# Causal attention in a fused transformer layer: one exp over a pair of key blocks

## The chip, the cores and the metric

The kernel runs on eight NeuronCores of one Trainium2 chip, each with one sequence of the batch. A core has a matmul engine (TensorE, PE in the profile, PEld for its weight loads), a vector engine (DVE), a scalar engine for activations (ACT), GpSimd (POOL), SyncE (SP), which issues DMAs, SBUF as working memory and PSUM with eight banks of 512 float32 columns per partition. Engines run their own queues in order and meet at semaphores. The metric is the device time in microseconds of the slowest core.

## What is computed

```python
def attn(x, W_query, W_key, W_value):          # x is layer-normed, 8 x 2048 x 1024, H = 16 heads, DH = 64
    q, k, v = ...                              # projections, split into heads
    scores = jnp.einsum('bhqd,bhkd->bhqk', q, k)
    scores = jnp.where(causal, scores, -jnp.inf)
    weights = jax.nn.softmax(scores / jnp.sqrt(jnp.float32(DH)), axis=-1)
    ctx = jnp.einsum('bhqk,bhkd->bhqd', weights, v)
    return ctx.transpose(0, 2, 1, 3).reshape(b, n, H * DH)

x = x + attn(layernorm(x), W_query, W_key, W_value)
x = x + ffn(layernorm(x), w1, conv_w, conv_b, w2)   # quantized linear, depthwise conv, silu, quantized linear
```

Each core works on one sequence of 2048 tokens.

## The kernel before

A first stage normalizes x and makes `qT`, `kT` and `vaug` (the values with a column of ones, which yields the row sums of softmax). The attention stage follows, from about 390 to 1010 us. The last stage is the feed-forward part.

In attention the loop over t (lines from 770) takes four query tiles of 512 rows; for tile t there are KC = 4t + 4 key blocks of 128. Within t, `hp` takes eight pairs of heads. For each key block `kc`, TensorE makes the scores of both heads with two matmuls (64 rows each, in the two halves of the array) into one half of the PSUM tensor `psS4`: `psS[kc % 2]`, two banks of four. ACT applies exp to this half (1024 columns, fewer on the four diagonal blocks, where columns above the diagonal are left out) and writes to `PT` in SBUF. The scores of kc wait for the exp of kc - 2, which read the same half. The first scores of a head pair also wait for the last matmuls of the previous pair's product with the values, and stand behind them on TensorE's queue.

After the exps of a head pair, DVE multiplies the diagonal blocks by a mask (eight instructions), TensorE multiplies `PT` by `vaug` into `psPV` (called PV here; 52, 84 and 116 matmuls for t = 1, 2, 3), and DVE divides by the row sums and adds to `x1st`, the residual rows of tile t. `x1st` is loaded by GpSimd's queue at the start of t and stored at its end; one buffer serves all tiles, so the load waits for the store.

Between head pairs `emit_wsteps(2)` adds two steps of the work on the feed-forward weights, in a fixed order: 16 steps of abs with a sum on ACT for w1, a finalize step (DVE and TensorE), 16 steps of abs for w2, another finalize step, then 16 + 16 steps of quantization on DVE (three instructions each). Each step has its own load into `wbuf` on SyncE's queue. A quantization step also stores its result on this queue, behind its own arithmetic and ahead of the load of the next step. Two steps a head pair put w1's abs into t = 0, w2's into t = 1, and quantization from head pair 1 of t = 2 on; two last steps come after the loop.

Every instruction goes through `Eng.emit` (line 75 in the profile). ACT and DVE have `chain=True`: each of their instructions waits for the end of the one before on its engine.

Of the kernel before, what the change touches and what calls it, by code (L numbers as in the profile page):

```python
# [10 lines left out]
AF = mybir.ActivationFunctionType  # L11
# [10 lines left out]
QTW = 512  # L22
# [109 lines left out]
def build_program(debug=False):  # L132
# [39 lines left out]
    with es:  # L172
# [14 lines left out]
        smalls = es.enter_context(nc.sbuf_tensor("smalls", [128, 64], F32))  # L187
# [7 lines left out]
        SE = Eng(nc.scalar, s_a, chain=True)  # L195
# [3 lines left out]
        toks = {}  # L199
# [12 lines left out]
        sec_s = sec("scalar")  # L212
# [237 lines left out]
        with esA2:  # L450
            PT = esA2.enter_context(nc.sbuf_tensor("PT", [128, 4 * 16 * 512], BF16))
            PTW = 16 * 512
# [5 lines left out]
            psS4 = esA2.enter_context(nc.psum_tensor("psS4", [128, 2048], F32))  # L458
# [313 lines left out]
            for t in range(NQT):  # L772
# [15 lines left out]
                for hp in range(8):  # L788
                    hA, hB = 2 * hp, 2 * hp + 1

                    for kc in range(KC):
                        hpar = kc % 2

                        @sec_t
                        def _(te, t=t, hp=hp, kc=kc, hpar=hpar, KC=KC,
                              q0=q0):
                            if kc >= 2:
                                TE.wait(toks[("exp", t, hp, kc - 2)])
                            elif hp >= 1:
                                TE.wait(toks[("exp", t, hp - 1, KC - 2 + kc)])  # L800
                            elif t >= 1:
                                TE.wait(toks[("exp", t - 1, 7, 4 * t - 2 + kc)])
                            if kc == 0:
                                if hp >= 1:
                                    TE.wait(toks[("pv", t, hp - 1, 1)])
                                elif t >= 1:
                                    TE.wait(toks[("pv", t - 1, 7, 1)])
                            TE.wait(toks["qkv_done_v"])
                            bP = psS[hpar]
                            TE.emit("matmul", bP[:, 0:QTW],  # L810
                                    kT[0:64, hp * S + 128 * kc:hp * S + 128 * (kc + 1)],
                                    qT[0:64, hp * S + q0:hp * S + q0 + QTW],
                                    start=True, stop=True,
                                    tile_position=(0, 0),
                                    skip_group_check=True)
                            TE.emit("matmul", bP[:, QTW:2 * QTW],
                                    kT[64:128, hp * S + 128 * kc:hp * S + 128 * (kc + 1)],
                                    qT[64:128, hp * S + q0:hp * S + q0 + QTW],
                                    start=True, stop=True,
                                    tile_position=(64, 0),  # L820
                                    skip_group_check=True)
                            toks[("sc", t, hp, kc)] = TE.tok()

                        @sec_s
                        def _(se, t=t, hp=hp, kc=kc, hpar=hpar, q0=q0):
                            SE.wait(toks[("sc", t, hp, kc)])
                            SE.wait(toks["expbias"])
                            if kc == 0:
                                if hp >= 2:
                                    SE.wait(toks[("pv", t, hp - 2, 0)])  # L830
                                    SE.wait(toks[("pv", t, hp - 2, 1)])
                                elif t >= 1:
                                    SE.wait(toks[("pv", t - 1, 6 + hp, 0)])
                                    SE.wait(toks[("pv", t - 1, 6 + hp, 1)])
                            c0 = max(0, (kc - 4 * t) * 128)
                            bP = psS[hpar]
                            src_ap = bP[:].rearrange(
                                "p (h w) -> p h w", w=QTW)[:, :, c0:QTW]
                            PTp = PT[:, (hp % 2) * 2 * PTW:
                                      (hp % 2 + 1) * 2 * PTW]  # L840
                            dst_ap = PTp.rearrange(
                                "p (h w) -> p h w", w=16 * 512)[
                                :, :, 512 * kc + c0:512 * (kc + 1)]
                            toks[("exp", t, hp, kc)] = SE.emit(
                                "activation", out=dst_ap, in_=src_ap,
                                func=AF.Exp, scale=0.125,
                                bias=smalls[:, 6:7])

                    PTp_A = PT[:, (hp % 2) * 2 * PTW:
                               (hp % 2) * 2 * PTW + PTW]  # L850
                    PTp_B = PT[:, (hp % 2) * 2 * PTW + PTW:
                               (hp % 2 + 1) * 2 * PTW]

                    @sec_v
                    def _(ve, t=t, hp=hp, PTp_A=PTp_A, PTp_B=PTp_B):
                        for j in range(4):
                            kc = 4 * t + j
                            VE.wait(toks[("exp", t, hp, kc)])
                            for P in (PTp_A, PTp_B):
                                sl = P[:, 512 * kc + 128 * j:512 * kc + 128 * (j + 1)]  # L860
                                VE.emit("tensor_tensor", sl, sl, maskt[:],
                                        ALU.mult)
                        toks[("mask", t, hp)] = VE.tok()

                    for hi, (head, P) in enumerate(((hA, PTp_A),
                                                    (hB, PTp_B))):
                        pv = psPV[hi]

                        @sec_t
                        def _(te, t=t, hp=hp, hi=hi, head=head, P=P, pv=pv):  # L870
                            if hp >= 1:
                                TE.wait(toks[("epi", t, hp - 1, hi)])
                            elif t >= 1:
                                TE.wait(toks[("epi", t - 1, 7, hi)])
                            TE.wait(toks[("exp", t, hp, 4 * t + 3)])
                            TE.wait(toks[("mask", t, hp)])
                            first = True
                            for m in range(4):
                                for kc in range(4 * t + m + 1):
                                    last = (m == 3) and (kc == 4 * t + 3)  # L880
                                    TE.emit(
                                        "matmul", pv[:, VW * m:VW * m + VW],
                                        P[:, 512 * kc + 128 * m:512 * kc + 128 * (m + 1)],
                                        vaug[:, kc * H * VW + head * VW:
                                             kc * H * VW + (head + 1) * VW],
                                        start=first, stop=last,
                                        skip_group_check=True)
                                    first = False
                            toks[("pv", t, hp, hi)] = TE.tok()

                        @sec_v
                        def _(ve, t=t, hp=hp, hi=hi, head=head, pv=pv,
                              xpar=xpar):
                            VE.wait(toks[("pv", t, hp, hi)])
                            VE.wait(toks[("x1_load", t)])
                            rs = pv[:, 0:4 * VW].rearrange(
                                "p (m w) -> p m w", w=VW)[:, :, DH:DH + 1]
                            VE.emit("reciprocal", recb[:, 0:4], rs)
                            for m in range(4):
                                xsl = x1st[:, m * D + head * DH:  # L900
                                           m * D + (head + 1) * DH]
                                VE.emit("scalar_tensor_tensor", xsl,
                                        pv[:, VW * m:VW * m + DH],
                                        recb[:, m:m + 1], xsl,
                                        ALU.mult, ALU.add)
                            toks[("epi", t, hp, hi)] = VE.tok()

                    emit_wsteps(2)
# [633 lines left out]
```

How the kernel before makes its waits and increments, by code:

```python
    def wait(self, tok):  # L52
        if tok is None:
            return
        if isinstance(tok, list):
            for t in tok:
                self.wait(t)
            return
        sem, val = tok
        if val <= 0:
            return
        key = id(sem)
        if self._waited.get(key, -1) >= val:
            return
        if not DRY[0]:
            self.raw.wait_ge(sem, val)
        self._waited[key] = val
# [1 line left out]
    def emit(self, name, *a, waits=(), **kw):  # L69
        if self.chain and self.n > 0:
            self.wait((self.sem, self.n))
        for t in waits:
            self.wait(t)
        if not DRY[0]:
            inst = getattr(self.raw, name)(*a, **kw)
            inst.then_inc(self.sem, 1)
        self.n += 1
        return (self.sem, self.n)
# [20 lines left out]
    def wait(self, tok):  # L99
        if tok is None:
            return
        if isinstance(tok, list):
            for t in tok:
                self.wait(t)
            return
        sem, val = tok
        if val <= 0:
            return
        key = id(sem)
        if self._waited.get(key, -1) >= val:
            return
        if not DRY[0]:
            self.raw.wait_ge(sem, val)
        self._waited[key] = val
# [1 line left out]
    def emit(self, name, *a, waits=(), **kw):  # L116
# [5 lines left out]
        if not DRY[0]:  # L122
            inst = getattr(self.raw, name)(*a, **kw)
            inst.then_inc(self.sems[j], 16)
        self.counts[j] += 16
```

## Time and profile before

| | us |
|---|---|
| median of the runs | 2216.52 (2216.39 to 2216.64) |
| profiled execution | 2218.43 |
| its span, slowest core (core 1) | 2216.9 |
| spans of the eight cores | 2198.3 to 2216.9 |
| mean granted TensorE clock | 0.703 to 0.711 of full speed |

Busy shares of the span on core 1 are 50% for matmuls, 48% for DVE, 37% for ACT and 13% for GpSimd. A timeline row reads: start, duration, engine, instruction with what it writes and reads, its count, and in brackets how long the engine sat idle before it and what ended this. A row with a count merges instructions that follow each other, with the gaps between them in its duration.

### The profile page before, as it was taken

Reading aid. Unit: us, or ns where it says so; the run is one execution under the profiler, and the core shown is the slowest. Engines: PE = TensorE matmul, PEld = TensorE weight load, DVE = VectorE, ACT = ScalarE, POOL = GpSimd, SP = SyncE. Lnnn points to the kernel's source line nnn. Section 1 sums busy time; section 2 is a strip of 40 time slices with the busy share of each in tenths; the row PEclk is TensorE's granted clock in tenths of the full one; section 3 lists DMA queues with packets and bytes.
Section 4 is the critical chain, followed back from the end, with each engine's and each line's share of the span. In section 5 each row is a group of like instructions: output and inputs, shape, how many; then the busy total and the mean of one; then the engine's idle time right before and its main releaser. Section 6 shows DMA issues by size and latency. Waiting matters only on the chain.

```text
span 2216.9 us, 23771 instructions; the slowest of 8 cores (2198.3 to 2216.9 us)
## 1 busy us (share of the span) xinstructions
PE 1100.4 (50%) x7038; PEld 600.2 (27%) x7038; DVE 1058.7 (48%) x2042; ACT 829.2 (37%) x904; POOL 281.7 (13%) x255
## 2 busy tenths in 40 slices
PE   0666784435444345551032346447364373757655
PEld 0322330113222222221021223324233242344422
DVE  1344444423245555554454645636456465566660
ACT  3100000858654445661133253261532524352522
POOL 0000000000000000000011321313213122142420
PEclk9977895555655556665566668668787687878787
DMA  7211001564523353334722131321313213141400
GB/s 215 73 38 39 19 18 59 200 199 152 190 69 123 123 167 113 117 118 168 239 95 86 49 112 48 123 67 59 120 51 124 67 58 105 57 152 58 133 19 19
DMA packets 108273, 224.03 MB, mean 101 GB/s; under 512 B 4593, under 2 KB 70258, under 8 KB 104050
## 3 DMA queue, kind: packets, MB, share of 16 engines
q1 hardware_dynamic: 94962, 172.18, 24.1%
q0 software_dynamic: 13184, 50.34, 6.4%
q8 instruction: 58, 0.95, 0.2%
q14 instruction: 69, 0.57, 0.1%
HBM read 188.94 MB, written 33.55 MB: 100 GB/s over the span
## 4 chain that ended last, share of the span: by engine, by line
DVE 34%; PE 24%; DMA 15%; ACT 15%; issue 9%; DVEq 1%; SPq 0%; ACTq 0%; POOL 0%; POOLq 0%
PE psQK L75 8%; PE psO L75 6%; DVE amx L75 5%; DVE t1s L75 5%; PE psPV L75 4%; DVE hsil L75 4%; DVE smalls L75 4%; DMA wbuf<-w1t 4%; ACT PT L75 4%; PE psM L75 3%; ACT hf L75 3%; DMA x1t<-x1scr 3%; DVE tmpc L75 3%; DVE cbuf L75 3%; DMA wbuf<-w2t 2%
## 5 line engine op out<-in xcount | busy, mean ns | idle before, releaser
L75 PE MATMUL psM<-xqT,t1b 128*128 128x258 bf16 x2048 | 334.4, 334 | 363.8 <-DVE cbuf L75 355.7
L75 ACT ACTIVATE PT<-psS,smalls 128x1024 bf16<-128x1024 f32 (+1 forms) x320 | 315.5, 986 | 227.8 <-PE psS L75 198.3
L75 PEld LDWEIGHTS psM<-xqT,t1b 128*128 128x128 bf16 x2048 | 235.8, 119 | 461.5 <-issue 394.2
L75 ACT ACTIVATE tmpc<-psM,convb_s,convw_s 128x256 f32<-128x256 f32 x256 | 144.5, 565 | 385.9 <-PE psM L75 254.6
L75 PE MATMUL psS<-qT,kT 64*128 64x512 bf16 x640 | 174.2, 548 | 192.4 <-ACT PT L75 186.7
L75 PE MATMUL psO<-t2T,hq 128*128 128x512 bf16 x1024 | 225.0, 382 | 35.1 <-ACT hq L75 35.1
L75 DVE SCALAR_TENSOR_TENSOR tmpc<-psM,convw_s,tmpc 128x256 f32<-128x256 f32 x256 | 123.7, 483 | 233.2 <-ACT tmpc L75 211.6
L75 POOL TENSOR_TENSOR hsil<-cbuf,hsil 128x1024 f32<-128x1024 f32 x64 | 150.7, 2354 | 541.8 <-ACT hsil L75 541.8
L75 PE MATMUL psPV<-vaug,PT 128*128 128x65 bf16 x2176 | 113.6, 234 | 117.5 <-DVE PT L75 117.5
L75 ACT ACT_TABLE_LOAD x26 | 33.4, 1283 | 302.4 <-DVE smalls L75 174.7
L75 PEld LDWEIGHTS psPV<-vaug,PT 128*128 128x128 bf16 x2176 | 110.0, 126 | 132.7 <-issue 132.7
L75 PEld LDWEIGHTS psO<-t2T,hq 128*128 128x128 bf16 x1024 | 100.2, 98 | 158.6 <-issue 41.2
L75 DVE SCALAR_TENSOR_TENSOR cbuf<-psM,convw_s,tmpc 128x256 f32<-128x256 f32 x256 | 123.7, 483 | 27.1 <-DVE tmpc L75 0.5
L75 PEld LDWEIGHTS psS<-qT,kT 64*128 64x128 bf16 x640 | 38.5, 100 | 316.1 <-issue 316.1
L75 DVE TENSOR_REDUCE amx<-hsil 128x256 f32<-128x8192 f32 x8 | 112.7, 14088 | 4.7 <-POOL hsil L75 3.9
L75 DVE TENSOR_TENSOR PT<-PT,mask_s 128x128 bf16<-128x128 bf16 x256 | 57.6, 225 | 102.8 <-ACT PT L75 80.2
L75 DVE TENSOR_SCALAR t1s<-wbuf,smalls 128x2048 bf16<-128x2048 f32 x32 | 41.1, 1286 | 125.4 <-DMA wbuf<-w2t 62.1
L75 DVE TENSOR_TENSOR hsil<-hsil,s2row 128x256 f32<-128x256 f32 x128 | 92.5, 723 | 14.1 <-DVE hsil L75 0.9
L75 POOL TENSOR_TENSOR hsil<-hsil,s2row 128x256 f32<-128x256 f32 x128 | 93.9, 734 | 40.6 <-DVE s2row L75 22.4
L75 ACT ACTIVATE smalls<-smalls 128x1 f32<-128x1 f32 x64 | 13.0, 203 | 229.4 <-DVE smalls L75 225.9
L75 ACT ACTIVATE hsil<-cbuf 128x1024 f32<-128x1024 f32 x64 | 67.6, 1056 | 54.3 <-DVE cbuf L75 52.1
L123 POOL DMA_DIRECT2D x1scr<-x1st x4 | 3.8, 945 | 652.4 <-DVE x1st L75 652.4
(80 smaller groups left out, 1173.1 us busy)
## 6 DMA issues: line engine op xcount, KB each, us to landing
t1b<-t1scr SPq DMA_DIRECT2D x64, 1024.0 KB, 5.4
wbuf<-w1t SPq DMA_DIRECT2D x32, 1024.0 KB, 6.3
wbuf<-w2t SPq DMA_DIRECT2D x32, 1024.0 KB, 6.0
xstage<-x POOLq DMA_DIRECT2D x16, 512.0 KB, 3.6
x1st<-x POOLq DMA_DIRECT2D x4, 2048.0 KB, 10.3
x1scr<-x1st POOLq DMA_DIRECT2D x4, 2048.0 KB, 10.1
t1scr<-t1s SPq DMA_DIRECT2D x16, 512.0 KB, 3.4
t2scr<-t1s SPq DMA_DIRECT2D x16, 512.0 KB, 3.2
```

Of the source, the lines that this page charges most:

```text
L75: inst = getattr(self.raw, name)(*a, **kw)
L123: inst = getattr(self.raw, name)(*a, **kw)
```

## The change

For key blocks off the diagonal (kc + 1 < 4t), two neighbours are taken together. The scores of kc and kc + 1 are emitted one behind the other, in the same halves as before, and one exp over both halves (2048 columns, all four banks of `psS4`) waits for both and writes both blocks of `PT`. Both exp tokens are set to this one instruction. Diagonal blocks keep one exp each. There are 2, 4 and 6 such pairs in a pair of heads for t = 1, 2, 3, and none for t = 0.

```diff
-                    for kc in range(KC):
+                    def emit_sc(t, hp, kc, KC, q0):
                         hpar = kc % 2
...
+                    def emit_exp2(t, hp, kc):
+                        @sec_s
+                        def _(se, t=t, hp=hp, kc=kc):
+                            SE.wait(toks[("sc", t, hp, kc)])
+                            SE.wait(toks[("sc", t, hp, kc + 1)])
+                            exp_pvwaits(t, hp, kc)
+                            src_ap = psS4[:].rearrange(
+                                "p (x h w) -> p h x w", x=2, h=2, w=QTW)
+                            PTp = PT[:, (hp % 2) * 2 * PTW:
+                                      (hp % 2 + 1) * 2 * PTW]
+                            dst_ap = PTp.rearrange(
+                                "p (h w) -> p h w", w=16 * 512)[
+                                :, :, 512 * kc:512 * (kc + 2)]
+                            dst_ap = dst_ap.rearrange(
+                                "p h (x w) -> p h x w", w=QTW)
+                            tok = SE.emit(
+                                "activation", out=dst_ap, in_=src_ap,
+                                func=AF.Exp, scale=0.125,
+                                bias=smalls[:, 6:7])
+                            toks[("exp", t, hp, kc)] = tok
+                            toks[("exp", t, hp, kc + 1)] = tok
+
+                    kc = 0
+                    while kc < KC:
+                        if kc + 1 < 4 * t:
+                            emit_sc(t, hp, kc, KC, q0)
+                            emit_sc(t, hp, kc + 1, KC, q0)
+                            emit_exp2(t, hp, kc)
+                            kc += 2
+                        else:
+                            emit_sc(t, hp, kc, KC, q0)
+                            emit_exp1(t, hp, kc)
+                            kc += 1
```

`emit_sc` and `emit_exp1` hold the former body of the loop, with its waits; `exp_pvwaits` holds the waits of the exp for the bias and, at kc = 0, for the PV of two head pairs before.

## Rows read from the trace of the kernel before

**Rows 1.** The page, chain that ended last, shares by line.
```profile
PE psQK L75 8%; PE psO L75 6%; DVE amx L75 5%; DVE t1s L75 5%; PE psPV L75 4%; DVE hsil L75 4%; DVE smalls L75 4%; DMA wbuf<-w1t 4%; ACT PT L75 4%; PE psM L75 3%; ACT hf L75 3%; DMA x1t<-x1scr 3%; DVE tmpc L75 3%; DVE cbuf L75 3%; DMA wbuf<-w2t 2%
```

**Rows 2.** Windows: stretch, length, busy us of PE, PEld, DVE, ACT, POOL, clock, DMA.
```profile
484.00:583.00 99.00, 54.24 (x486) 28.04 (x486) 33.65 (x139) 81.87 (x85) 0.00 (x0) 0.55 0.38 134
824.00:1017.00 193.00, 97.43 (x1032) 51.20 (x1032) 99.32 (x170) 115.11 (x112) 0.00 (x0) 0.62 0.34 115
```

**Rows 3.** Waits of the attention stage, 392 to 1063 us: total, times, longest.
```profile
ACT PT L75 <- PE psS L75: 198.3, 24, 19.6
PE psS L75 <- ACT PT L75: 186.7, 256, 3.5
```

**Rows 4.** Timeline of head pair 3 in t = 1, all engines.
```profile
516.21 1.03 PE L75 MATMUL psS<-qT,kT 64*128 64x512 bf16 x4
516.97 8.32 ACT L75 ACTIVATE PT<-psS,smalls 128x1024 bf16<-128x1024 f32 x8 [0.67 <-PE psS L75]
518.23 0.61 PE L75 MATMUL psS<-qT,kT 64*128 64x512 bf16 x2 [0.99 <-ACT PT L75]
524.86 1.21 DVE L75 TENSOR_TENSOR PT<-PT,mask_s 128x128 bf16<-128x128 bf16 x4 [0.23 <-ACT PT L75]
526.22 3.02 PE L75 MATMUL psPV<-vaug,PT 128*128 128x65 bf16 x52 [1.56 <-DVE PT L75]
```

**Rows 5.** Groups of instructions by form, ACT, attention stage: count, busy us, mean ns.
```profile
L75 ACT ACTIVATE PT<-psS,smalls 128x1024 bf16<-128x1024 f32 x224 | 249.6, 1114 | 216.8 <-PE psS L75 198.3
L75 ACT ACTIVATE wbuf<-wbuf 128x2048 f32<-128x2048 f32 x32 | 61.1, 1910 | 9.3 <-DMA wbuf<-w1t 7.1
L75 ACT ACTIVATE PT<-psS,smalls 128x512 bf16<-128x512 f32 x32 | 22.0, 687 | 3.0
L75 ACT ACTIVATE PT<-psS,smalls 128x256 bf16<-128x256 f32 x32 | 15.2, 474 | 4.2
```

**Rows 6.** Timeline of PE in t = 2 and t = 3.
```profile
624.87 3.90 PE L75 MATMUL psPV<-vaug,PT 128*128 128x65 bf16 x84 [1.56 <-DVE PT L75]
...
650.73 4.55 PE L75 MATMUL psPV<-vaug,PT 128*128 128x65 bf16 x84 [8.60 <-DVE PT L75]
...
822.74 0.61 PE L75 MATMUL psS<-qT,kT 64*128 64x512 bf16 x4 [0.19 <-PE psPV L75]
824.56 0.39 PE L75 MATMUL psS<-qT,kT 64*128 64x512 bf16 x2 [1.21 <-ACT PT L75]
...
844.99 5.65 PE L75 MATMUL psPV<-vaug,PT 128*128 128x65 bf16 x116 [4.35 <-DVE PT L75]
```

**Rows 7.** Timeline of DVE and ACT in t = 1 and t = 2.
```profile
484.01 0.18 DVE L75 RECIPROCAL recb<-psPV 128x4 f32<-128x4 f32 x1 [14.35 <-DMA x1st<-x]
...
490.61 8.32 ACT L75 ACTIVATE PT<-psS,smalls 128x1024 bf16<-128x1024 f32 x8 [19.63 <-PE psS L75]
...
621.73 0.56 DVE L75 TENSOR_TENSOR PT<-PT,mask_s 128x128 bf16<-128x128 bf16 x2 [11.07 <-ACT PT L75]
...
629.61 13.15 ACT L75 ACTIVATE PT<-psS,smalls 128x1024 bf16<-128x1024 f32 x12 [5.67 <-PE psS L75]
...
648.05 2.53 DVE L75 TENSOR_TENSOR PT<-PT,mask_s 128x128 bf16<-128x128 bf16 x8
```

**Rows 8.** Timeline of DVE and ACT in t = 3.
```profile
808.40 1.29 DVE L75 TENSOR_SCALAR t1s<-wbuf,smalls 128x2048 bf16<-128x2048 f32 x1 [12.86 <-DMA wbuf<-w1t]
...
823.30 17.98 ACT L75 ACTIVATE PT<-psS,smalls 128x1024 bf16<-128x1024 f32 x16 [16.16 <-PE psS L75]
...
842.31 2.53 DVE L75 TENSOR_TENSOR PT<-PT,mask_s 128x128 bf16<-128x128 bf16 x8
...
848.51 0.18 DVE L75 RECIPROCAL recb<-psPV 128x4 f32<-128x4 f32 x1 [3.67 <-PE psPV L75]
...
1004.42 2.29 ACT L75 ACTIVATE PT<-psS,smalls 128x768 bf16<-128x768 f32 x3 [0.37 <-ACT PT L75]
...
1006.66 2.53 DVE L75 TENSOR_TENSOR PT<-PT,mask_s 128x128 bf16<-128x128 bf16 x8
```

More of the change, by code:

```diff
@@ L822, in _, with exp_pvwaits, emit_exp1 @@
                             toks[("sc", t, hp, kc)] = TE.tok()
+                    def exp_pvwaits(t, hp, kc):
+                        SE.wait(toks["expbias"])
+                        if kc == 0:
+                            if hp >= 2:
+                                SE.wait(toks[("pv", t, hp - 2, 0)])
+                                SE.wait(toks[("pv", t, hp - 2, 1)])
+                            elif t >= 1:
+                                SE.wait(toks[("pv", t - 1, 6 + hp, 0)])
+                                SE.wait(toks[("pv", t - 1, 6 + hp, 1)])
+                    def emit_exp1(t, hp, kc):
+                        hpar = kc % 2
                         @sec_s
-                        def _(se, t=t, hp=hp, kc=kc, hpar=hpar, q0=q0):
+                        def _(se, t=t, hp=hp, kc=kc, hpar=hpar):
                             SE.wait(toks[("sc", t, hp, kc)])
[L827 to L834, printed above, removed]
+                            exp_pvwaits(t, hp, kc)
                             c0 = max(0, (kc - 4 * t) * 128)
@@ L847, in _ @@
                                 bias=smalls[:, 6:7])
+                    def emit_exp2(t, hp, kc):
[3 more added lines that the diff above has]
+                            SE.wait(toks[("sc", t, hp, kc + 1)])
+                            exp_pvwaits(t, hp, kc)
+                            src_ap = psS4[:].rearrange(
[24 more added lines that the diff above has]
+                            kc += 1
                     PTp_A = PT[:, (hp % 2) * 2 * PTW:
```

## The prediction

> **What bounds the kernel now.** I read first the page's chain of work that ended last [rows 1]: exp (`PT`) is only 4% of it. The change touches nothing outside the attention stage, so the question is what ends last there. The table of windows, cut by query tile t, has most of t = 1 and most of t = 3 [rows 2]: ACT is busy 82 of 99 us in the one but 115 of 193 in the other; TensorE was granted 0.55 and 0.62 of full speed, so mostly its lower level of 1.2 GHz. The waits of the stage [rows 3] show both directions of one hand-over: ACT waited 198 us for scores, PE 187 us for exps.
>
> The timeline of one head pair in t = 1 shows the unit [rows 4]. Four score matmuls (kc 0 and 1) start at 516.21; the exp of kc 0 starts at 516.97 without waiting for kc 1. It lasts 1.114 us [rows 5], so it ends at 518.08, and the matmuls of kc 2 start at 518.23: 0.15 us from exp to matmul. They take 0.61, while ACT already runs the exp of kc 1. The eight exps fill 8.32 us; their own durations sum to 7.63, so some 0.09 lies between two, and a full exp costs ACT 1.205. PE's work is hidden because two halves of `psS4` alternate.
>
> Which engine ends last differs by tile. In t = 1 the last exp ends at 525.29, the last mask at 526.07 (0.78 later), and PV starts at 526.22 [rows 4]; the next scores stand behind PV on PE. ACT's two abs jobs end before these scores arrive (ahead of 516.97 ACT has waited 0.67 for PE). Exps, masks and PV form the closed path. In t = 3 DVE's weight quantization ends last: a step, a load that SyncE issues only behind the store of this step, a second step, then the masks: in head pair 1 the exps ended at 841.28, and the masks, of which the first could have begun before that, started at 842.31 [rows 8]. Exps there have slack.
>
> **The change part by part.** It merges 96 pairs of full exps (2, 4, 6 a head pair in t = 1, 2, 3, times 8). Nothing changes in t = 0, in diagonal blocks, in masks, PV, DMAs or queues; the number of waits is the same or lower.
>
> *Duration of the merged exp.* The forms of 256, 512 and 1024 columns take 474, 687 and 1114 ns [rows 5]: 213.3 ns for each 256 columns and 260 ns fixed. 2048 columns give 1.97 us. Bounds: 1.91 (the abs over 2048 columns, no PSUM operand, same rows) and 2.23 (two exps, nothing saved). I take 1.97, which the line through three rows of the same operation gives. On ACT alone a pair falls from 2.41 to 2.06: 0.35 saved.
>
> *The lost overlap.* The merged exp reads all four banks. The scores of kc + 2 and kc + 3 both wait for it, and the next merged exp waits for both. PE and ACT now take turns. At the lower clock four score matmuls take 1.04 [rows 4], so a pair costs 1.97 + 0.15 + 1.04 + 0.15 = 3.31 us against 2.41: +0.90. At the upper clock four take 0.61 and two 0.39 [rows 6]: 1.97 + 0.15 + 0.61 + 0.15 = 2.88, +0.47. The first merged exp of a head pair waits for four matmuls instead of two (+0.43 low, +0.22 high), and the first diagonal exp waits for its own scores (0.15 + 0.61 + 0.15 = 0.91 instead of 0.09). Summed for a head pair with n merged exps, low clock: first 1.04 + 0.15, then 1.97n + 1.34(n - 1) + 0.91, against 0.76 + 2.41n. That is +1.80 for n = 2, +3.60 for n = 4, +5.40 for n = 6. In t = 3 the first four matmuls behind PV ran at the upper clock (0.61 for four, the exp 0.56 behind their start) [rows 6, 8], so there I use 0.77 and 0.56 as starts: 0.77 + 11.82 + 6.70 + 0.91 - 0.56 - 14.46 = +5.18.
>
> I take the lower clock elsewhere: with a score pair every 1.2 us the pair takes 0.61, its lower-clock time, in the middle of a head pair [rows 4], and with the change PE works 1.04 in 3.31 us instead of 0.61 in 1.205.
>
> The Trainium skill, PSUM — Partial Sum Buffer, section Summary: rules for kernel authors, says that PSUM read while a matmul runs should be a different bank. This change leaves scores no different bank; by the rule, as by the waits, the hand-over is on the path.
>
> *t = 1.* Head pair 0 is hidden: DVE waited 14.35 us for the `x1st` load until 484.01, and ACT, whose scores stood on PE behind the first finalize, 19.63 us until 490.61 [rows 7]. The other seven follow one path from there. 7 x 1.80 = 12.6.
>
> *t = 2.* Head pair 0 is hidden again behind the load of `x1st`, in the same pattern. Head pair 1 is not: DVE idled 11.07 us for its exps: +3.6. For head pairs 2 to 7, six alike, the last exp ended at 642.76; masks bound by it would end 0.78 later at 643.54, and they ended at 650.58 behind quantization [rows 7]. Slack 7.0, at most 3.6 needed: 0. This cover would cost 6 x 3.6 = 21.6 if it were gone.
>
> *t = 3.* Head pair 0 stands behind a load for which DVE waited 12.86 us [rows 8]: 0. The remaining seven: slack is mask end less (last exp end + 0.78). First: 844.84 - (841.28 + 0.78) = 2.78; last: 1009.19 - (1006.71 + 0.78) = 1.70 [rows 8]. The seven are 2.78, 1.91, 2.48, 2.20, 2.31, 2.11, 1.70: 15.5 in all. 7 x 5.18 - 15.5 = 20.8. The masks of these head pairs become exp-bound; quantization, behind them on DVE, starts later by as much, and the last two quantization steps shift the following stage.
>
> *PV.* PV of t = 2 took 4.55 us behind 8.60 us of idle PE, and 3.90 behind 1.56 [rows 6]. In t = 3 it follows 4.35 us idle now [rows 6] and will follow some 1.6. Between 0 and 7 x 0.65 = 4.6 gained; I take 2, since part of that idle time is gone already.
>
> Sum: 12.6 + 3.6 + 20.8 - 2 = +35.0 us. The profiled execution took 2218.4 (span 2216.9), which gives 2253.4; it stood 1.9 above the median of 2216.5, which gives 2251.5, +1.6%. Its own range goes from 2243 to 2260.
>
> **The rivals.**
> *Scores at the upper clock.* Then 0.95 for each head pair of t = 1 (6.6), 1.9 for head pair 1 of t = 2, 2.9 less 2.2 slack for seven of t = 3 (4.8): +13.3, less up to 4.6 for PV: +9 to +13, about 2228. For it: scores just behind PV run fast. Against: the others don't. 0.14.
> *Nothing saved by the wide exp.* If it takes 2.23 us, 0.26 x 60 pairs on the path (14, 4, 42) adds 15.6: 2267, slower by over 2%. The three forms lie on one line, which speaks against it, but no row has a four-bank read. Any 0.16 us more on each of 60 pairs passes the 2% border. 0.16 for ends above the border.
> *t = 3 stays with DVE.* If loads run longer and slack exceeds 5.2, only 16.2 is left: 2233. The row of 12.86 us waiting for a load shows that they can; but one of eight. 0.04.
> *The other side: PE at full speed throughout.* PV would cost 38 ns a matmul (the second half of the 116 in t = 3: 58 between 848.5, where DVE went on with the first half, and the end at 850.6 [rows 6, 8]), 1.0 less for each of 7 in t = 1 (52 in 3.02 now [rows 4]), 0.7 in t = 2, 1.25 for each of 7 in t = 3: -16.4. With +13.3: -3, 2213. It decides only if the clock stays up in nearly all of the stage; PE gets sparser, so 0.03.
> *ACT is the bound and the saving counts.* If PE could work under the merged exp, 0.35 x 18 pairs outside t = 3 would be gained: -6, 2210. The waits for scores speak against it: 0.02. The Trainium skill, Perfetto Trace Analysis, section Optimizing Scalar/DVE Operations, says grouping into larger operations can help where the engine is saturated, and that where it is not and leaves bubbles elsewhere, breaking up may finish sooner. The trace has ACT waiting 198 us for PE, so it agrees with the second sentence.
>
> **How the numbers follow.** 0.61 for the forecast, the others as given. A change under 2% (44 us) can't be told from none here. Slower by over 2% has the 0.16; faster by over 2% (below 2172) has no case, 0.01 for the unknown; the rest, 0.83, lies within. The range from 2226 to 2264 takes in the upper-clock case and that of t = 3 with DVE; it leaves out the two cheapest cases (0.05) and the part of the dear one above 2264 (0.10).
>
> **What would show it.** `PT` activations of 128x2048 x96 near 1.97 us; ACT busy less by some 25 us (96 x 0.26) though the stage is longer; scores mostly in fours, 1.04 us, starting 3.3 apart; ACT's wait for scores up by some 100 us; t = 1 longer by 12 to 13, t = 2 by 3 to 4, t = 3 by about 20, with masks there waiting for exps; nothing moved in the stages around. Wrong: a wide exp outside 1.91 to 2.1, scores at 0.61 in fours in the middle of a head pair, or t = 2 longer by 20.

## The result and the profile after

The changed kernel took 2254.8 us (median) beside 2220.7 of the kernel before in the same runs: 1.015 times as long, 95% interval 1.013 to 1.018, so 28 to 39 us more. Its profiled execution took 2251.4 with a span of 2249.9 on core 5. Medians are over all executions; ratios and their intervals leave out a few that took 1 to 2% longer, with the cores of one die at a lower granted clock.

The page's line on the chain that ended last, shares by line, now begins with the exps (they had 4% in [rows 1]):

```profile
ACT PT L75 8%; PE psQK L75 8%; PE psO L75 6%; DVE amx L75 5%; PE psPV L75 4%; DVE hsil L75 4%; DVE smalls L75 4%; DMA wbuf<-w1t 3%; PE psS L75 3%; ACT hf L75 3%; DMA x1t<-x1scr 3%; DVE t1s L75 3%; DVE tmpc L75 3%; DVE cbuf L75 3%; PE psM L75 2%
```

The merged form among the groups of ACT's instructions in the attention stage (count, busy us, mean ns, idle before), and the waits of this stage (total, times, longest), which answer to [rows 3, 5]:

```profile
L75 ACT ACTIVATE PT<-psS,smalls 128x2048 bf16<-128x2048 f32 x96 | 189.0, 1969 | 256.7 <-PE psS L75 256.6
```

```profile
ACT PT L75 <- PE psS L75: 280.8, 120, 20.5
PE psS L75 <- ACT PT L75: 277.3, 160, 4.0
```

96 instructions of 1.97 us, as the line through the narrow forms gave. ACT's busy time of the whole span fell by 23 us (829.2 to 805.8), and both directions of waiting grew, ACT's for scores by 83 us and PE's for exps by 91. ACT in one head pair of t = 1, to be laid beside [rows 4, 7]:

```profile
507.89 1.97 ACT L75 ACTIVATE PT<-psS,smalls 128x2048 bf16<-128x2048 f32 x1 [1.09 <-PE psS L75]
511.19 1.97 ACT L75 ACTIVATE PT<-psS,smalls 128x2048 bf16<-128x2048 f32 x1 [1.34 <-PE psS L75]
514.07 3.50 ACT L75 ACTIVATE PT<-psS,smalls 128x1024 bf16<-128x1024 f32 x4 [0.91 <-PE psS L75]
...
525.75 1.97 ACT L75 ACTIVATE PT<-psS,smalls 128x2048 bf16<-128x2048 f32 x1 [0.92 <-PE psS L75]
```

Between merged exps ACT is idle for 1.34 us, and starts are 3.30 apart. The first diagonal exp waits 0.91. Some gaps are 0.92, the time that four scores need at the upper clock: over all cores, in head pairs 1 to 7, 23 of the 56 gaps between merged exps in t = 1, 27 of 168 in t = 2 and 17 of 280 in t = 3.

PE in t = 3: a turn of four score matmuls, then PV (compare [rows 6]), and DVE between its two quantization steps and the masks (compare [rows 8]):

```profile
905.54 1.03 PE L75 MATMUL psS<-qT,kT 64*128 64x512 bf16 x4 [2.27 <-ACT PT L75]
908.85 1.04 PE L75 MATMUL psS<-qT,kT 64*128 64x512 bf16 x4 [2.27 <-ACT PT L75]
...
893.21 5.88 PE L75 MATMUL psPV<-vaug,PT 128*128 128x65 bf16 x116 [1.56 <-DVE PT L75]
```

```profile
884.85 2.29 DVE L75 TENSOR_TENSOR t1s<-t1s,wbuf 128x2048 bf16<-128x2048 bf16 x1
890.07 0.55 DVE L75 TENSOR_TENSOR PT<-PT,mask_s 128x128 bf16<-128x128 bf16 x2 [2.93 <-ACT PT L75]
```

PE stands idle for 2.27 us of each 3.31. Quantization is done at 887.14, and the masks now wait 2.93 us for exps, where before they followed it at once. Head pairs 1 to 7 of t = 3 on core 5 in both kernels (stretch, length, busy us of PE, PEld, DVE, ACT, POOL, granted clock, DMA share, GB/s), first after, then before:

```profile
838.00:1047.00 209.00, 91.26 (x923) 44.41 (x920) 97.71 (x163) 105.00 (x70) 0.00 (x0) 0.56 0.32 106
```

```profile
819.00:1003.00 184.00, 90.11 (x916) 44.26 (x916) 97.14 (x160) 115.67 (x112) 0.00 (x0) 0.62 0.34 115
```

The same work takes 209 us instead of 184, with 105 us of ACT's time instead of 116.

Since a core's absolute times shift by some us with its loads, the comparisons below go by parts of the attention stage, from exp start to exp start in the timelines, as means over the eight cores of the profiled execution (h = head pair):

| us | t=1, h 1-7 | t=2, h 1 | t=2, h 2-7 | t=3, h 0 | t=3, h 1-6 | t=3, exps of h 7 |
|---|---|---|---|---|---|---|
| before | 92.0 | 19.2 | 160.5 | 32.8 | 164.5 | 18.3 |
| after | 102.0 | 22.9 | 160.1 | 32.1 | 183.6 | 22.9 |
| only_t1 | 101.7 | 19.4 | 161.0 | 32.6 | 165.8 | 18.0 |
| only_t2 | 92.3 | 22.5 | 160.4 | 32.0 | 164.3 | 18.0 |
| only_t3 | 92.0 | 19.3 | 161.4 | 33.1 | 184.3 | 22.9 |
| turns_narrow | 108.2 | 24.4 | 161.5 | 32.5 | 194.4 | 24.7 |
| fill_wide | 95.6 | 20.9 | 160.1 | 31.9 | 163.9 | 20.6 |
| early_load_narrow | 92.0 | 19.3 | 118.8 | 25.4 | 153.4 | 18.3 |
| early_load_wide | 101.8 | 22.9 | 135.1 | 30.1 | 183.8 | 22.9 |
| early_load_fill2 | 89.9 | 19.2 | 116.0 | 23.9 | 147.4 | 18.2 |

The profiled execution of only_t3 took 2256.9, 20 above the median of its runs. As a mean of its cores t = 1 starts 7 us late and 5 more pass behind the last mask, both outside the parts of the table.

### The profile page after: what moved, and what is told of

It reads as the page before. It is cut to its first block, busy times and chain, and to the rows that moved or that the text cites. A ratio compares the mean times of both kernels' runs of the same rounds, so it can differ in the third digit from the quotient of the medians.

```text
span 2249.9 us, 23483 instructions; the slowest of 8 cores (2234.7 to 2249.9 us)
## 1 busy us (share of the span) xinstructions
PE 1088.7 (48%) x7038; PEld 592.9 (26%) x7038; DVE 1059.4 (47%) x2042; ACT 805.8 (36%) x808; POOL 281.7 (13%) x255
## 4 chain that ended last, share of the span: by engine, by line
DVE 31%; PE 27%; ACT 19%; DMA 11%; issue 10%; DVEq 1%; ACTq 0%; SPq 0%; POOL 0%; POOLq 0%
ACT PT L75 8%; PE psQK L75 8%; PE psO L75 6%; DVE amx L75 5%; PE psPV L75 4%; DVE hsil L75 4%; DVE smalls L75 4%; DMA wbuf<-w1t 3%; PE psS L75 3%; ACT hf L75 3%; DMA x1t<-x1scr 3%; DVE t1s L75 3%; DVE tmpc L75 3%; DVE cbuf L75 3%; PE psM L75 2%
## 5 line engine op out<-in xcount | busy, mean ns | idle before, releaser
L75 ACT ACTIVATE PT<-psS,smalls 128x1024 bf16<-128x1024 f32 (+2 forms) x224 | 291.0, 1299 | 291.6 <-PE psS L75 280.8
L75 PE MATMUL psS<-qT,kT 64*128 64x512 bf16 x640 | 160.4, 568 | 282.7 <-ACT PT L75 277.3
L75 PE MATMUL psO<-t2T,hq 128*128 128x512 bf16 x1024 | 223.6, 381 | 35.8 <-ACT hq L75 35.8
L75 PEld LDWEIGHTS psS<-qT,kT 64*128 64x128 bf16 x640 | 28.7, 102 | 402.5 <-issue 402.4
```

What stands on the lines that cost most here:

```text
L75: inst = getattr(self.raw, name)(*a, **kw)
```

## The experiments

**Each tile alone.** The condition of the merge gets a term for t, here for t = 3:

```diff
-                        if kc + 1 < 4 * t:
+                        if t == 3 and kc + 1 < 4 * t:
```

> Merged exps in t = 1 alone. Theory A: head pairs 1 to 7 of t = 1 take 102 instead of 92 us, everything else as before: +10, near 2228. Rival (ACT's abs work sets t = 1 and a shorter exp helps it): 92 or less.

> Merged exps in t = 2 alone. Theory A with cover: head pair 1 takes 22.9 instead of 19.2 us, head pairs 2 to 7 stay at 160.5: +3.6, near 2222. Rival (no cover): head pairs 2 to 7 take 182, +25 in all.

> Merged exps in the last query tile (t = 3) alone; t = 1 and 2 as before. Theory A with slack (2.2 us a head pair behind quantization absorb a part of 5.2): head pairs 1 to 7 of t = 3 take 206 instead of 183 us, to the mask end 22 more; whole kernel +22, near 2241, 1.0% above before. Rival (no slack counts): 7 x 5.2 = +36. Rival (hidden behind quantization): 0.

Measured ratios to the kernel before: only_t1 1.0035 (1.0003 to 1.0066), only_t2 1.002 (0.997 to 1.007), only_t3 1.0086 (1.005 to 1.012). The parts are sharper. only_t1 lengthens t = 1 by 9.7 us and nothing in t = 2. only_t2 lengthens head pair 1 by 3.2 and leaves the other six where they were, 160.4 beside 160.5: the cover is there. only_t3 adds 19.8 to six periods and 4.6 to the last exps, of which 1.5 were slack as a mean of the cores: 22.9. The three parts make 9.7 + 3.2 + 22.9 = 35.8, all of the loss. Of the whole-kernel ratios only_t2's can't be told from none. ACT's abs work doesn't rule t = 1 (it does once PV gets shorter, see below), and in t = 3 quantization absorbs a part, neither none nor all.

**The turns without the wide exp.** Two exps of 1024 columns in place of one, both behind all four scores; the next scores wait for the second.

```diff
-                            emit_exp2(t, hp, kc)
+                            emit_exp1(t, hp, kc, kc + 1)
+                            emit_exp1(t, hp, kc + 1, kc + 1)
+                            alias_exp(t, hp, kc)
```

> Four score matmuls, then two exps of 1024 columns which both wait for all four, then the next four matmuls behind the second exp: the turns of the changed kernel, without its wide exp. Theory A (taking turns costs, the wide exp gives back 0.35 us a pair): a pair takes 1.114 + 0.09 + 1.114 + 0.15 + 1.04 + 0.15 = 3.66 us instead of 3.31, some 60 pairs on the path, so 21 us above the changed kernel: near 2276, 2.4 to 2.7% above the kernel before. Rival B (the wide exp over four banks is itself what costs): with narrow exps the time goes back to about that of the kernel before, 2217 to 2230.

It took 2275.5 us, ratio 1.027 (1.022 to 1.033), where 2276 was expected. ACT in t = 1:

```profile
509.09 2.32 ACT L75 ACTIVATE PT<-psS,smalls 128x1024 bf16<-128x1024 f32 x2 [1.10 <-PE psS L75]
512.75 2.32 ACT L75 ACTIVATE PT<-psS,smalls 128x1024 bf16<-128x1024 f32 x2 [1.34 <-PE psS L75]
```

The pair of exps takes 2.32 us, then the same 1.34 of idle time, 3.66 from start to start. So the loss is in the turns, and the wide exp gives back 0.35 a pair: without it the kernel is some 21 us slower still. The rival that put the cost on the wide exp, 2217 to 2230, is out.

**The cover taken away.** In the quantization steps the load of step i + 1 goes to SyncE's queue ahead of the store of step i. The load waits for step i - 1, whose half of `wbuf` it fills.

```diff
+                qloads.append(load)
+
                 def f():
+                    if i == 0:
+                        qloads[0]()
+                    qloads[i + 1]()
+
                     @sec_v
                     def _(ve):
                         VE.wait(toks[("w1q_dma", i)])
```

> The kernel before, with SyncE's queue in another order in the quantization steps: the load of step i + 1 is issued ahead of the store of step i (it waits for step i - 1, whose buffer it takes), so DVE needn't wait some 6.7 us between its two steps. Exps narrow as before. Theory: quantization no longer ends last; head pairs 2 to 7 of t = 2 become 6 x 6.7 = 40 us shorter, those of t = 3 only 7 x 2.2 = 15 (then the exps end last), and the tail behind attention loses two or three such waits, 10 to 15: 65 to 75 less, near 2147 (ratio 0.968). Rival: loads and stores then compete, and the wait stays: under 20 less.

> The same early loads under the changed kernel (merged exps). If the change was cheap in t = 2 only because quantization covered it, the cover is gone now: against early_load_narrow +10 in t = 1, 7 x 3.6 = 25 in t = 2, 8 x 5.2 = 42 and some 3 for slower PV in t = 3: +75 to +80, near 2225. Rival (merged exps cost the same with or without that cover, as a fixed loss): +35 against early_load_narrow, near 2182.

early_load_narrow took 2139.4 us, ratio 0.967 (0.961 to 0.973): 79 us less by medians, 73 by the ratio, where 65 to 75 was expected and the rival said under 20. DVE in t = 2 goes from one step to the next and on to the masks with no load to wait for, where it waited 6.60 in the kernel before (first row):

```profile
642.87 1.29 DVE L75 TENSOR_SCALAR t1s<-wbuf,smalls 128x2048 bf16<-128x2048 f32 x1 [6.60 <-DMA wbuf<-w1t]
...
694.18 2.29 DVE L75 TENSOR_TENSOR t1s<-t1s,wbuf 128x2048 bf16<-128x2048 bf16 x1
696.58 1.29 DVE L75 TENSOR_SCALAR t1s<-wbuf,smalls 128x2048 bf16<-128x2048 f32 x1
697.97 1.28 DVE L75 TENSOR_SCALAR wbuf<-wbuf,smalls 128x2048 f32<-128x2048 f32 x1
699.36 2.29 DVE L75 TENSOR_TENSOR t1s<-t1s,wbuf 128x2048 bf16<-128x2048 bf16 x1
701.76 2.53 DVE L75 TENSOR_TENSOR PT<-PT,mask_s 128x128 bf16<-128x128 bf16 x8
```

Head pairs 2 to 7 of t = 2 lost 41.7 us, as expected; six periods of t = 3 lost 11.1, or 1.9 each, the slack less a slower PV. Head pair 0 of t = 3 lost another 7.3, and the stretch behind the last mask 17, more than the 10 to 15 expected.

early_load_wide took 2209.6, 70 us above early_load_narrow where the merge had cost 34 before; the expectation was 75 to 80, the rival's 35: the fixed loss is out, and the expectation was some 5 too high. The parts: 9.8 in t = 1, 3.6 in head pair 1, 16.3 in the other six of t = 2, 4.6 in head pair 0 of t = 3, 30.4 + 4.6 behind it, and -1.4 in head pair 0 of t = 2. The 16.3 are short of 6 x 3.6 = 21.6, or 0.9 a head pair, for several reasons. In the narrow kernel the masks still follow quantization without a wait (last row above), but they end only 0.3 later than exps alone would let them. The exps grew by 2.9 instead of 3.2, some gaps being 0.92. The first exp came 0.2 later behind its scores instead of 0.4, and PV was 0.1 shorter. So what the change costs is set by what else ends late, not by the edit: 3.2 us a pair of heads in t = 3 are 5.1 once the cover is gone.

**The clock.** Matmuls are added whose results nobody reads.

```diff
                             emit_sc(t, hp, kc + 1, KC, q0)
+                            emit_fill(t, hp, 4)
                             emit_exp2(t, hp, kc)
...
+                            for _i in range(n):
+                                TE.emit("matmul", psN[:, 0:512],
+                                        kT[:, 0:128], qT[:, 0:512],
+                                        start=True, stop=True)
```

> The changed kernel with matmuls added whose results nobody reads (into psN): four of 512 columns behind the scores of each merged exp, one behind the scores of each diagonal block, two behind the last. They run while ACT works on the merged exp. Theory (half of what the lost overlap costs is TensorE's lower clock): the granted clock of the stage rises towards 1.0, four scores take 0.61 instead of 1.04, a pair 2.88 instead of 3.31, and PV gets shorter (3.0 to some 2.2 in t = 1, 5.8 to some 4.5 in t = 3): t = 1 about 10 shorter, t = 3 about 25 shorter, whole kernel near 2220. Rival (the clock stays low all the same, and the added matmuls only stand in the way where ACT ends first): 2255 to 2262.

fill_wide took 2229.8, ratio 1.003 (0.9995 to 1.006) to the kernel before, so 25 us less than the changed kernel by medians and 28 by ratios; near 2220 was expected. A window of t = 3 in the changed kernel, the same window in fill_wide, and ACT and PE in it:

```profile
860.00:960.00 100.00, 47.49 (x555) 27.14 (x556) 45.16 (x83) 46.31 (x33) 0.00 (x0) 0.57 0.32 106
...
860.00:960.00 100.00, 62.37 (x685) 30.14 (x685) 52.11 (x94) 53.43 (x38) 0.00 (x0) 0.97 0.34 117
...
899.51 1.97 ACT L75 ACTIVATE PT<-psS,smalls 128x2048 bf16<-128x2048 f32 x1 [0.92 <-PE psS L75]
902.40 1.97 ACT L75 ACTIVATE PT<-psS,smalls 128x2048 bf16<-128x2048 f32 x1 [0.92 <-PE psS L75]
...
904.51 0.61 PE L75 MATMUL psS<-qT,kT 64*128 64x512 bf16 x4 [1.31 <-ACT PT L75]
905.05 1.04 PE L75 MATMUL psN<-qT,kT 128*128 128x512 bf16 x4
```

Granted clock 0.97 instead of 0.57 (0.86 and 0.82 in windows of t = 1 and t = 2, instead of 0.56 and 0.58); four scores in 0.61; exps start every 2.89 us: the price of a turn at the upper clock that the prediction had as a rival. PV fell from 3.01 to 2.38 in t = 1 and from 5.84 to 4.56 in t = 3 (means over head pairs 1 to 7 of all cores). t = 1 got 6.4 shorter where 10 was expected, and is still 3.6 longer than before; t = 3 got 22 shorter where 25 was expected.

> Narrow exps and early loads, with two such added matmuls behind the scores of each full block, one behind those of a diagonal block and two behind the last. If the clock rises to the upper level for the stage: hand-over of scores stays hidden, PV shortens by 0.8 in t = 1 and 1.2 in t = 3 for each head pair, and the first exp comes 0.2 earlier: 15 to 25 below early_load_narrow, near 2120. If it stays at the lower level, three matmuls at 0.43 are longer than an exp with its gap (1.28 against 1.205), so some 0.1 a block is lost: near 2150.

early_load_fill2 took 2129.2, ratio 0.958 (0.955 to 0.961): 10 below early_load_narrow by medians and by the spans as a mean of the cores (2120 beside 2131), and the fastest of all. That is less than the 15 to 25 expected.

```profile
858.78 0.39 PE L75 MATMUL psS<-qT,kT 64*128 64x512 bf16 x2 [0.28 <-ACT PT L75]
859.11 0.60 PE L75 MATMUL psN<-qT,kT 128*128 128x512 bf16 x2
```

Scores at the upper clock, 0.39, with the added pair behind them and the exps' spacing of 1.21 kept. PV shortened as expected or more, by 0.9 in t = 1 and 1.6 in t = 3. But seven times 0.9 took only 2.0 us off t = 1, and in t = 3 only 1.0 a head pair came off. Scores and ACT in t = 1 show where the gain stopped:

```profile
514.25 0.39 PE L75 MATMUL psS<-qT,kT 64*128 64x512 bf16 x2 [0.35 <-PE psPV L75]
...
515.21 0.19 ACT L75 ACTIVATION_READ_ACCUMULATOR wbuf<-wbuf 128x1 f32 x1
...
515.49 8.28 ACT L75 ACTIVATE PT<-psS,smalls 128x1024 bf16<-128x1024 f32 x8
```

The scores are done at 514.64, and the first exp starts at 515.49, 0.09 behind ACT's second abs step, without idle time: with a shorter PV the abs work on ACT ends last here, as in 33 of the 56 head pairs 1 to 7 of all cores; in t = 1 of fill_wide it does in 24, in the kernels before and after in none. In t = 3 quantization ends last again in head pair 1 (its masks end 2.9 us after the exps would let them), and 0.25 more passes between PV and the next scores.

## Why the prediction was right

2251.5 was forecast and 2254.8 measured; +1.6% and +1.5%. The turns, the cover in t = 2 and the slack in t = 3 came out as worked out. The PV term had the wrong sign and two terms were a little off; that the sums agree to 1 us is partly luck, since these errors had opposite signs.

*The merged exp.* 1.97 us forecast, 1.97 measured, x96.

*The turn.* +0.90 a pair at the lower clock: starts 3.31 apart, gap 1.34, first diagonal exp 0.91 late, each as computed. turns_narrow separates its two parts: +1.25 for the turn, -0.35 for the wide exp.

*t = 1: 12.6 forecast, 10.0 measured.* The step "I take the lower clock elsewhere" was too plain: a head pair of t = 1 has one gap between merged exps, and in 23 of 56 it was 0.92 instead of 1.34; the first exp came 0.28 later behind its scores instead of 0.43. 1.43 a head pair instead of 1.80.

*t = 2: 3.6 forecast, 3.6 measured* in head pair 1, and -0.5 where 0 was forecast for the six covered ones. That the cover was real is shown by only_t2, and that it was the quantization by early_load_wide.

*t = 3: 20.8 without the PV term, 18.8 with it; 22.2 measured* for head pairs 1 to 7 (19.1 in six periods, 4.6 less 1.5 of slack at the last), and -0.7 in head pair 0. The slack was rightly read: head pairs wait for exps now, and only_t3 gave 22.9. The PV term had the wrong sign. The step "PV of t = 2 took 3.90 behind 1.56 us of idle time" took the idle time ahead of PV for what sets its speed. Against that stands t = 2 of early_load_wide: PV behind 1.56 of idle time took 4.50 there, as long as the 4.52 of the kernel before behind 7.8 (both means over head pairs and cores). PV of head pairs 1 to 7 of t = 3 went from 5.46 to 5.84 us; six of them lie ahead of the last mask, 2.3 more instead of 2 less. With that the term without PV is 19.9 instead of 20.8. The granted clock of the stretch fell from 0.62 to 0.56 while scores got sparser. Read inside PV alone (head pairs 1 to 6 of t = 3, all cores) it was 0.64 before, 0.59 after, 0.85 in fill_wide and 0.92 in early_load_fill2, and PV took 5.44, 5.83, 4.49 and 4.07; so PV's time follows the clock. What exactly delays its rise inside PV isn't settled.

*The sum.* 10.0 + 3.6 - 0.5 + 22.2 = 35.3, and +0.7 and -0.7 in head pairs 0 of t = 2 and t = 3: 35.3 to the last mask. As a mean of the cores the spans of the profiled executions differ by 35.6, on the slowest core by 33.0, the medians by 34.1; 35.0 was forecast. t = 1 came out 2.6 under the forecast and t = 3 3.4 over it, which cancelled.

*The rivals.* Nothing saved by the wide exp: out, 1.97. t = 3 stays with DVE: out, by the masks' wait of 2.93. Scores at the upper clock, and PE at full speed throughout: not in this kernel, but fill_wide made much of the case. Its interval, 1 us less to 13 more than the kernel before, takes in the +9 to +13 worked out for the one and not the -3 of the other. PV gained less there than 38 ns a matmul would give (4.56 us for 116 is 39 ns, but in t = 1 2.38 for 52 is 46). And the second rival's 1.0 less for each head pair of t = 1 overlooked ACT's abs work, which often ends last when PV is that short: of 0.9 less in early_load_fill2, 0.3 came off. ACT as the bound: out, it waits 83 us more. The sentence of the Trainium skill, Perfetto Trace Analysis, section Optimizing Scalar/DVE Operations, that grouping helps a saturated engine has its condition unmet here; that smaller instructions may end sooner where the engine leaves bubbles is what the two kernels show, though not by their size alone: in turns_narrow the small ones, held to the same turns, are slower than the wide one.

## What to carry to other kernels

Merging two instructions over both halves of a double buffer ends the double buffering: weigh the saved fixed cost (here 0.35 us a pair) against the producer's whole time plus two hand-overs (1.34, or 1.25 net of the 0.09 between two exps), and count only head pairs or tiles where this engine ends last. Read for each stage which wait ends last before pricing an edit, and which comes next: a PV shorter by 0.9 us gave 0.3 in t = 1, where ACT's abs work stood right behind it; the same edit cost 34 us here and 70 once a store no longer stood ahead of a load on a queue. Where two engines take turns, look first at the queue that isn't under discussion: its order was worth 73 to 79 us.

## What the runs showed of the hardware

- An exp over four PSUM banks through a four-dimensional access pattern costs nothing extra here: 1.97 us for 2048 columns, on the line of 256 to 1024 columns (474, 687 and 1114 ns).
- Four filler matmuls per turn held the granted clock at 0.97 in a window of t = 3 where it had been 0.57, and shortened the kernel by 25 us; fillers in the fastest version gave 10.
- At one and the same count of 116 matmuls, PV took between 4.10 us (early_load_fill2) and 5.84 (after) as a mean of head pairs 1 to 7, with a granted clock inside PV of 0.92 and 0.59.
- A load that stands behind a store on SyncE's queue waits for the arithmetic that the store waits for: 6.6 to 7.1 us between two quantization steps, and none when the load was issued first.
